# A transformer block and a graph attention on one core: three small attention products put side by side behind the up projection

## The chip, the cores and the metric

The kernel runs on one core of a Trainium2 chip. The metric is the device time of one launch in microseconds (us). Five engines of the core take part, each with its own queue of instructions in program order: TensorE (PE in the rows; its weight loads are PEld), VectorE (DVE), ScalarE (ACT), GpSimd (POOL), and SyncE (SP), which issues the DMAs. They meet only through semaphores.

## What is computed

128 sequences of 64 positions and 256 features go through two layers. All is float32; large products are made in pieces (below).

```python
# layer 0, per sequence
x_mod = rms(x) * (1 + scale_msa) + shift_msa
q, k, v = split(x_mod @ qkv_w)                   # 16 heads of 16
q, k = rope(rms(q) * lnq_w), rope(rms(k) * lnk_w)
attn = softmax(q @ k.T / 4)                      # 64 x 64 per head
x = x + gate_msa * (attn @ v @ proj_w + proj_b)
h = rms(x) * (1 + scale_mlp) + shift_mlp
x = x + gate_mlp * ((silu(h @ w1_w) * (h @ w3_w)) @ w2_w)   # 704 wide
# layer 1
sf = concat(x, where(x.sum(-1) == 0, 0, cond)) @ W_self.T + b_self
for d in range(2):                               # two directions
    aff = q1 @ k1.T / 4                          # keys: the first 20 positions
    w = softmax(where(mask, aff, NEG) + label_bias)
    out += w @ kv @ Wout[d] + bout[d]
y = x + relu(sf + out)
```

## The kernel before, in words

The 8192 rows are cut into 32 blocks of 256 positions (4 sequences); in most steps a block has two tiles `t` of 128 positions. Each engine runs a hand-written list of steps, `ORDER` (line 80), once per iteration of a loop over blocks. An entry `(a, step, n)` means: do part `n` of `step` for block `m + a`. So one iteration works on four blocks at once: `a = 3` is the youngest (norm and qkv), `a = 2` its first attention, `a = 1` projection and MLP, `a = 0` the graph attention, called the second attention here (its functions end in 1). `run_steps` (line 151) writes out the first four and the last three iterations and loops over the others. A block's work goes through all engines: for `qkv`, for instance, TensorE makes the product, ScalarE squares q and k (`qk_sq`) and copies v (`vb`), VectorE makes the two rotary products `qs` and `qc`, sums the squares, and adds `qr`.

Products of full precision take two parts of each operand, made as high (ScalarE copy to fp32r: `nh`, `gh`, `aoh`) and low part (the difference, on GpSimd: `nl`, `gl`; `aol` on VectorE). `linear` (line 483) writes their matmuls, so that their rows all have line 486.

Three kinds of TensorE work use a part of the array. `mix` (line 612; rows L622) multiplies transposed probabilities of the first attention with `v`, in tiles of 64 columns, 32 matmuls for each `t`. `mix1` (line 797; rows L806) does this for the second attention in tiles of 32 columns, also 32. `score`, `score1` and `v1` are tiled too and are not touched. Probabilities come from VectorE and ScalarE, are transposed by TensorE (`probs_t`, L607; `probs_t1`, L792), and copied to SBUF by ScalarE: to `pT0` for the first attention and to `pT1` for the second, one buffer each, used for both tiles in turn.

PSUM has 8 banks; `BANK` (line 72) says which product goes to which. Before a product overwrites a bank, TensorE waits for those who read what was in it (`wait_free`, line 139: a list of signals, each with a block offset and a count; the first whose block exists is waited for).

Other steps that the prediction names: TensorE `mixT` (L631, transposes the mixed values, the last but one step of an iteration), `heads` (L570, transposes q and k), `self` (the second layer's linear map, whose low part reads `nl` from `x2_split`), `mlp_down` in two parts. VectorE `mix` (L1162 reciprocal and L1165, divides by the sums), `qkv` (L1118, L1120, L1124, twice L1130), `mlp_up` (L1192, L1195, L1197, L1201), `mix1` (L1276), `edges` (L1221), `rope_scale` (L1135), `out` (L1282), `rope` (L1141), `mlp_down` (L1206, writes `x`). ScalarE `mlp_split` (L926, writes `gh`), `rope_scale` (L886, a square root, for which it loads a table). GpSimd `mlp_down` (L1360, adds to `x`), `heads` (L1327, `kbd`), `x2_split` (L1315, `nl`), `mlp_up` (L1315, `gl`). GpSimd's list ends `mlp_down`, `heads` 0, `x2_split`, `heads` 1, and VectorE's begins `rope` 0, `rope` 1, `mlp_down`.

The functions that the diff touches, with their lines:

Of the kernel before, what the change touches and what calls it, by code (L numbers as in the profile page):

```python
# [27 lines left out]
P = 128  # L28
# [45 lines left out]
    "mix": (5, 6), "q1": (4, 6), "score": 0, "score1": 0, "mixT": 6, "proj": 2, "norm1": 7, "up": (6, 4, 6),  # L74
# [10 lines left out]
        (1, "mlp_up", 1), (3, "qkv", 0), (0, "probsT1", 0), (2, "mix", 1), (3, "qkv", 1), (0, "mix1", 0),  # L85
        (0, "probsT1", 1), (1, "mlp_up", 2), (0, "mix1", 1), (1, "mlp_down", 0), (1, "mlp_down", 1), (2, "mixT", 0),
# [9 lines left out]
        (1, "mlp_up", 1), (2, "mix", 1), (3, "qkv", 0), (3, "qkv", 1), (1, "mlp_up", 2), (0, "mix1", 0),  # L96
# [8 lines left out]
        (0, "probsT1", 0), (3, "qkv", 0), (1, "mlp_split", 1), (3, "qkv", 1), (0, "probsT1", 1), (1, "mlp_up", 2),  # L105
# [64 lines left out]
def build_program(nc, d):  # L170
    with ExitStack() as ctx:
# [67 lines left out]
        pT0, pT1 = pT[:, 0, :, :], pT[:, 1, :, :]  # L239
# [242 lines left out]
        def _(pe):  # L482
# [129 lines left out]
            def mix(m, t):  # L612
# [3 lines left out]
                if t == 0:  # L616
                    wait_free(pe, m, (pT_a, 0, 1))
                elif t == 1:
                    wait_free(pe, m, (z_silu, -1, 1), (normed[0], 1, 1))
# [16 lines left out]
            def proj(m, n):  # L636
                first_use(m, "proj")
                wait(pe, mixed_hi, m, 1)
                wait_free(pe, m, (cos_part, 1, 1), (biased1, -2, 4))
# [7 lines left out]
            def mlp_up(m, n):  # L647
# [6 lines left out]
                for name, out in (("w1", z_ps[n]), ("w3", u_ps[n])):  # L654
# [8 lines left out]
                    elif (n, name) == (2, "w1"):  # L663
                        wait_free(pe, m, (mix_normed, 1, 2), (z_silu, 0, 1))
# [132 lines left out]
            def mix1(m, t):  # L797
# [5 lines left out]
                for j in range(NJ):  # L803
                    for s in range(2):
                        f = 32 * (j % 4)
                        last = nc.tensor.matmul(ao1_ps[f:f + 32, j // 4, t * P + s * S:t * P + (s + 1) * S],  # L806
                                                vb1[:, 2 * t + s, :, j], pT1[:, j, s * S:(s + 1) * S],
# [11 lines left out]
        def _(act):  # L819
# [47 lines left out]
            def qkv(m, t):  # L867
                wait(act, qkv_done, m, t + 1)
                qk_ps, v_ps = qkv_ps[t]

                wait(act, qk_sums, m, t)
                nc.scalar.activation(qk_sq[:, :, :, :].rearrange("p a h f -> p (a h f)"), qk_ps, ACT.Square)\
                    .then_inc(qk_squares.sem, 1)
                if t == 0:
                    wait_last(act, mixed, m)
                v = v_ps.rearrange("p (j h f) -> p j h f", h=2, f=DH)
# [561 lines left out]
```

## Time and profile before

| | |
|---|---|
| median of 3 runs | 1422.27 us (1420.46 to 1423.88) |
| span of the profiled execution, first to last instruction | 1416.1 us |
| what lies around the span, median less span | 6.2 us |
| granted TensorE clock, mean over the span | 0.977 |
| TensorE matmul busy | 1342.2 us (95%) |
| VectorE busy | 1135.2 us (80%) |
| ScalarE busy | 878.6 us (62%) |
| GpSimd busy | 712.1 us (50%) |
| DMA | 56.19 MB, mean 40 GB/s |

The timed executions and the profiled one are different executions; the span is what the rows below come from. Busy TensorE is the union of its matmuls, whose ends are modelled. The granted clock is at full speed from about the fourth block to the last; the slices before it are partly at half of that. Busy shares say how full an engine is, not whether something waits for it: for this the rows of a single block are needed.

### The profile page before, as it was taken

The numbers are of one execution on the slowest core, as the hardware profiler recorded it, in microseconds if no ns is written. First come the engines' busy times: TensorE is split into PE (matmuls) and PEld (weight loads), VectorE is DVE, ScalarE is ACT, GpSimd is POOL, SyncE is SP. The second block draws the span as 40 slices with busy tenths as digits, with TensorE's granted clock in tenths as the row PEclk, the third lists the DMA queues.
The fourth block names the chain that finished last, engine by engine and source line by source line (L and its number), as shares of the span: only waits on it lengthen the run. The fifth ranks groups of instructions, "written<-read, shape, count | busy, mean of one in ns | idle before, by whom it ended". The sixth has DMA issues, their size and how long they took to land.

```text
span 1416.1 us, 51305 instructions
## 1 busy us (share of the span) xinstructions
PE 1342.2 (95%) x20276; PEld 1229.1 (87%) x20276; DVE 1135.2 (80%) x2033; ACT 878.6 (62%) x1752; POOL 712.1 (50%) x612
## 2 busy tenths in 40 slices
PE   4679999999999999999999999999999999999985
PEld 3578899999998999999898999999999999999974
DVE  5667888888888888888888888888888888888753
ACT  4556666666666666666666666666666666656542
POOL 0235555455655544555555455555545555554541
PEclk8589999999999999999999999999999999999998
DMA  7001111010111101111110111111011111100100
GB/s 240 29 23 30 45 43 43 18 38 30 43 43 43 43 15 36 34 43 43 43 43 15 35 35 43 43 43 43 15 33 37 43 43 43 43 15 28 30 22 16
DMA packets 49827, 56.19 MB, mean 40 GB/s; under 512 B 4352, under 2 KB 47744, under 8 KB 49792
## 3 DMA queue, kind: packets, MB, share of 16 engines
q1 hardware_dynamic: 48944, 53.86, 12.1%
q10 hardware_dynamic: 848, 1.84, 0.4%
q8 instruction: 25, 0.41, 0.1%
q14 instruction: 10, 0.08, 0.0%
HBM read 47.03 MB, written 8.65 MB: 39 GB/s over the span
## 4 chain that ended last, share of the span: by engine, by line
PE 73%; issue 9%; POOL 7%; ACT 3%; DVE 1%; ACTq 0%; POOLq 0%; DVEq 0%
PE psum L486 39%; PE psum L607 5%; PE psum L622 5%; PE psum L728 4%; PE psum L792 4%; PE psum L758 4%; PE psum L775 3%; POOL nl L1315 3%; PE psum L587 3%; PE psum L806 2%; POOL gl L1315 2%; POOL kbd L1327 2%; ACT gh L926 1%; PE psum L534 1%; ACT qkT L892 1%
## 5 line engine op out<-in xcount | busy, mean ns | idle before, releaser
L1315 POOL TENSOR_TENSOR gl<-gf,gh 128x512 fp32r<-128x512 f32 x96 | 124.3, 1295 | 260.4 <-ACT gh L926 260.4
L486 PE MATMUL psum<-nh,w_lo 128*128 128x256 f32 x704 | 182.2, 289 | 0.0
L486 PE MATMUL psum<-nh,w_hi 128*128 128x256 f32 x704 | 176.8, 282 | 0.0
L1315 POOL TENSOR_TENSOR nl<-xn,nh 128x512 fp32r<-128x512 f32 x64 | 99.2, 1551 | 127.3 <-ACT nh L864 127.3
L486 PEld LDWEIGHTS psum<-nh,w_lo 128*128 128x128 f32 x704 | 132.8, 189 | 1.0 <-issue 1.0
L486 PEld LDWEIGHTS psum<-nh,w_hi 128*128 128x128 f32 x704 | 133.0, 189 | 0.0
L1379 POOL TENSOR_TENSOR e<-e,inv 128x640 f32<-128x640 f32 x64 | 82.0, 1282 | 87.6 <-DVE inv L1271 87.6
L486 PE MATMUL psum<-nl,w_hi 128*128 128x256 f32 x704 | 115.4, 282 | 0.0
L926 ACT ACTIVATE gh<-gf 128x512 fp32r<-128x512 f32 x96 | 60.3, 628 | 61.6 <-DVE gf L1201 60.8
L486 PEld LDWEIGHTS psum<-nl,w_hi 128*128 128x128 f32 x704 | 97.5, 188 | 0.0
L486 PE MATMUL psum<-qkv_lo,nh 128*128 128x512 f32 (+1 forms) x256 | 88.5, 356 | 2.8 <-ACT nh L864 2.8
L946 ACT ACTIVATE sf<-psum,colb 128x256 f32<-128x256 f32 x64 | 26.8, 470 | 103.3 <-PE psum L486 103.3
L1151 DVE TENSOR_REDUCE mx<-psum 128x16 f32<-128x1024 f32 x64 | 78.1, 1221 | 14.4 <-PE psum L587 14.1
L911 ACT ACTIVATE aoh<-psum 128x512 fp32r<-128x512 f32 x32 | 19.1, 598 | 109.2 <-PE psum L631 109.2
L486 PE MATMUL psum<-gh,w_lo 128*128 128x256 f32 x320 | 83.0, 290 | 1.3 <-ACT gh L926 1.3
L486 PE MATMUL psum<-qkv_hi,nh 128*128 128x512 f32 (+1 forms) x256 | 82.4, 343 | 0.0
L607 PE MATMUL psum<-ident,e 128*128 128x128 f32 x512 | 77.9, 289 | 4.3 <-ACT e L897 4.2
L1360 POOL TENSOR_TENSOR x<-x 128x512 f32<-128x512 f32 x32 | 41.5, 1296 | 78.2 <-DVE x L1206 78.2
L1327 POOL TENSOR_TENSOR kbd<-qkT,hmask 128x512 f32<-128x512 f32 x64 | 66.5, 1041 | 28.0 <-ACT qkT L892 28.0
L486 PE MATMUL psum<-gh,w_hi 128*128 128x256 f32 x320 | 79.6, 279 | 0.0
L1156 DVE TENSOR_TENSOR e<-psum,mx 128x1024 f32<-128x1024 f32 x64 | 78.0, 1218 | 1.3
L622 PEld LDWEIGHTS psum<-vb,pT 128*64 128x64 f32 x2048 | 66.6, 140 | 12.8 <-issue 12.5
(186 smaller groups left out, 4382.4 us busy)
## 6 DMA issues: line engine op xcount, KB each, us to landing
adj<-in_adj SPq DMA_DIRECT2D x32, 440.0 KB, 3.3
x_in<-in_x SPq DMA_DIRECT2D x32, 256.0 KB, 2.7
xn<-in_xT SPq DMA_DIRECT2D x32, 256.0 KB, 3.6
x_res<-in_xT SPq DMA_DIRECT2D x32, 256.0 KB, 3.7
out_T<-y SPq DMA_DIRECT2D x32, 256.0 KB, 2.2
e<-in_adaln ACTq DMA_DIRECT2D x2, 512.0 KB, 5.4
stage<-in_qkv SPq DMA_DIRECT2D x2, 384.0 KB, 5.0
pT<-in_w SPq DMA_DIRECT2D x2, 384.0 KB, 6.4
```

Of the source, the lines that this page charges most:

```text
L486: last = nc.tensor.matmul(out, lhsT, rhs, start=start and i == 0, stop=stop and i == len(terms) - 1)
L607: last = nc.tensor.transpose(pT_out[t][j // 4][:, j % 4, :], e0[t][:, 2 * pair(j):2 * pair(j) + 2, :].rearrange("p h s -> p (h s)"), ident ...
L622: last = nc.tensor.matmul(mix_ps[t][s * S:(s + 1) * S, j, :], pT0[:, j, s * S:(s + 1) * S], vb[:, t, s, j, :], start=True, stop=True, tile ...
L728: last = nc.tensor.matmul(k1_out[:, k, :].rearrange("p (b k) -> p b k", b=MB), wk1[:, c, k * P:(k + 1) * P], sf[:, c, :].rearrange("p (b s ...
L758: last = nc.tensor.matmul(v1_out[r * NKP:(r + 1) * NKP, b, :], kv[:, c, b, :], wo1[:, c, r * P:(r + 1) * P], start=c == 0, stop=c == DC - ...
L792: last = nc.tensor.transpose(pT1_out[t][j // 4][:, j % 4, :], e1[t][:, 2 * pair(j):2 * pair(j) + 2, :, :].rearrange("p h a k -> p (h a k)" ...
L926: nc.scalar.activation(gh[:, 2 * n:2 * n + 2, :], gf[:, :, :], ACT.Copy).then_inc(g_hi.sem, 1)
L1151: nc.vector.tensor_reduce(mx0_v, s_v[t], AX.X, ALU.max).then_inc(maxima.sem, 1)
L1156: nc.vector.tensor_tensor(e0_v[t], s_v[t], mx0_v.unsqueeze(3).to_broadcast([P, NG, 4, S]), ALU.subtract).then_inc(shifted_s.sem, 1)
L1315: return nc.gpsimd.tensor_tensor(out, full, hi.bitcast(F32), ALU.subtract)
L1327: nc.gpsimd.tensor_tensor(kbd[:, t, :, :, :, :].rearrange("p c s h k -> p (c s) h k"), qkT[t][:, 1, :, :].rearrange("p c (s k) -> p (c s) ...
L1379: nc.gpsimd.tensor_tensor(e_v, e_v, inv1[t][:, :].unsqueeze(2).to_broadcast([P, ND * H, NKV]), ALU.mult)\
```

## The change

In TensorE's list the second `mix` (tile 1 of the first attention) and both `mix1` move behind the last part of the up projection, so that the three follow each other. For this the transposed probabilities of the second attention get a second buffer, `mix` 1 writes bank 2 in place of bank 6, and the waits before reuse of banks follow. VectorE's `mix` 1 moves from before `qkv` to behind the last `mlp_up`. On ScalarE the copies of v leave `qkv` and become a step of their own, `values`: tile 0's stays behind `qkv` 0, tile 1's comes last in the list, since it may overwrite `vb` only when the `mix` of the block before has read it. There `qkv` 1 also changes places with `probsT1` 1.

```diff
@@ -71,7 +71,7 @@
 
 BANK = {
     "xT": 6, "qk": (2, 3), "v": (7, 1), "heads": (7, 5), "probsT": (5, 4, 4, 0), "probsT1": (0, 5, 4, 7),
-    "mix": (5, 6), "q1": (4, 6), "score": 0, "score1": 0, "mixT": 6, "proj": 2, "norm1": 7, "up": (6, 4, 6),
+    "mix": (5, 2), "q1": (4, 6), "score": 0, "score1": 0, "mixT": 6, "proj": 2, "norm1": 7, "up": (6, 4, 6),
     "gate": (3, 1, 0), "down": 1, "rowsum": 3, "self": 4, "k1": 5, "v1": 7, "mix1": 5,
 }
 
@@ -82,8 +82,8 @@
         (2, "heads", 1), (1, "proj", 0), (0, "self", 0), (0, "self_cond", 0), (2, "score", 0), (0, "k1", 0),
         (0, "q1", 0), (1, "norm1_mean", 0), (0, "q1", 1), (1, "norm1_apply", 0), (2, "probsT", 0),
         (3, "norm0_apply", 0), (0, "score1", 0), (0, "v1", 0), (2, "mix", 0), (2, "probsT", 1), (1, "mlp_up", 0),
-        (1, "mlp_up", 1), (3, "qkv", 0), (0, "probsT1", 0), (2, "mix", 1), (3, "qkv", 1), (0, "mix1", 0),
-        (0, "probsT1", 1), (1, "mlp_up", 2), (0, "mix1", 1), (1, "mlp_down", 0), (1, "mlp_down", 1), (2, "mixT", 0),
+        (1, "mlp_up", 1), (3, "qkv", 0), (0, "probsT1", 0), (3, "qkv", 1), (0, "probsT1", 1), (1, "mlp_up", 2),
+        (2, "mix", 1), (0, "mix1", 0), (0, "mix1", 1), (1, "mlp_down", 0), (1, "mlp_down", 1), (2, "mixT", 0),
         (3, "heads", 0),
     ],
     "DVE": [
@@ -93,7 +93,7 @@
         (3, "norm0_apply", 0), (3, "norm0_shift", 0), (0, "score1_bias", 0), (0, "score1_max", 0),
         (0, "score1_bias", 1), (0, "score1", 0), (2, "mix", 0), (0, "score1_max", 1), (0, "soft1", 0),
         (0, "soft1_inverse", 0), (1, "mlp_up", 0), (0, "score1", 1), (0, "soft1", 1), (0, "soft1_inverse", 1),
-        (1, "mlp_up", 1), (2, "mix", 1), (3, "qkv", 0), (3, "qkv", 1), (1, "mlp_up", 2), (0, "mix1", 0),
+        (1, "mlp_up", 1), (3, "qkv", 0), (3, "qkv", 1), (1, "mlp_up", 2), (2, "mix", 1), (0, "mix1", 0),
         (1, "edges", 0), (3, "rope_scale", 0), (0, "out", 0),
     ],
     "Activation": [
@@ -102,7 +102,8 @@
         (3, "norm0_mean", 0), (2, "score", 0), (0, "q1", 0), (0, "q1", 1), (2, "probsT", 0), (2, "score", 1),
         (1, "norm1_apply", 0), (0, "v1", 0), (3, "norm0_apply", 0), (1, "edges", 0), (0, "score1", 0),
         (2, "probsT", 1), (1, "mlp_up", 0), (1, "mlp_split", 0), (0, "score1", 1), (1, "mlp_up", 1),
-        (0, "probsT1", 0), (3, "qkv", 0), (1, "mlp_split", 1), (3, "qkv", 1), (0, "probsT1", 1), (1, "mlp_up", 2),
+        (0, "probsT1", 0), (3, "qkv", 0), (3, "values", 0), (1, "mlp_split", 1), (0, "probsT1", 1), (3, "qkv", 1),
+        (1, "mlp_up", 2), (3, "values", 1),
     ],
     "Pool": [
         (1, "proj", 0), (0, "self_split", 0), (3, "norm0_mean", 0), (1, "norm1_mean", 0), (1, "norm1_scale", 0),
@@ -236,7 +237,7 @@
         inv0 = [sb(f"inv0_{i}", [P, NJ, 2]) for i in range(TILES)]
         aon = [sb(f"aon{i}", [P, NJ, 2, DH]) for i in range(TILES)]
         pT = sb("pT", [P, 2, NJ, P])
-        pT0, pT1 = pT[:, 0, :, :], pT[:, 1, :, :]
+        pT0, pT1 = pT[:, 0, :, :], [pT[:, 1, :, :], sb("pT1_1", [P, NJ, P])[:, :, :]]
         aoh = sb("aoh", [P, DC, MT], F32R)
         aol = sb("aol", [P, DC, MT], F32R)
 
@@ -616,7 +617,7 @@
                 if t == 0:
                     wait_free(pe, m, (pT_a, 0, 1))
                 elif t == 1:
-                    wait_free(pe, m, (z_silu, -1, 1), (normed[0], 1, 1))
+                    wait_free(pe, m, (cos_part, 1, 1), (biased1, -2, 4), (shifted_s, 0, 2))
                 for j in range(NJ):
                     for s in range(2):
                         last = nc.tensor.matmul(mix_ps[t][s * S:(s + 1) * S, j, :], pT0[:, j, s * S:(s + 1) * S],
@@ -636,7 +637,7 @@
             def proj(m, n):
                 first_use(m, "proj")
                 wait(pe, mixed_hi, m, 1)
-                wait_free(pe, m, (cos_part, 1, 1), (biased1, -2, 4))
+                wait_free(pe, m, (mix_normed, 0, 2))
                 for o in both:
                     linear(proj_ps[:, o, :], high_terms("proj", out_chunks[o], aoh, both), o == 0, False)
                 wait(pe, mixed_lo, m, 1)
@@ -661,7 +662,7 @@
                     elif (n, name) == (1, "w3"):
                         wait_free(pe, m, (biased1, -1, 4), (shifted_s, 1, 2))
                     elif (n, name) == (2, "w1"):
-                        wait_free(pe, m, (mix_normed, 1, 2), (z_silu, 0, 1))
+                        wait_free(pe, m, (z_silu, 0, 1))
                     elif (n, name) == (2, "w3"):
                         wait_free(pe, m, (pT1_a, -1, 1), (pT_b, 1, 2))
                     for c, w, j in chunks[name]:
@@ -804,7 +805,7 @@
                     for s in range(2):
                         f = 32 * (j % 4)
                         last = nc.tensor.matmul(ao1_ps[f:f + 32, j // 4, t * P + s * S:t * P + (s + 1) * S],
-                                                vb1[:, 2 * t + s, :, j], pT1[:, j, s * S:(s + 1) * S],
+                                                vb1[:, 2 * t + s, :, j], pT1[t][:, j, s * S:(s + 1) * S],
                                                 start=True, stop=True, tile_position=(0, f))
                 last.then_inc(mixed1.sem, 1)
 
@@ -866,14 +867,14 @@
 
             def qkv(m, t):
                 wait(act, qkv_done, m, t + 1)
-                qk_ps, v_ps = qkv_ps[t]
-
                 wait(act, qk_sums, m, t)
-                nc.scalar.activation(qk_sq[:, :, :, :].rearrange("p a h f -> p (a h f)"), qk_ps, ACT.Square)\
+                nc.scalar.activation(qk_sq[:, :, :, :].rearrange("p a h f -> p (a h f)"), qkv_ps[t][0], ACT.Square)\
                     .then_inc(qk_squares.sem, 1)
-                if t == 0:
-                    wait_last(act, mixed, m)
-                v = v_ps.rearrange("p (j h f) -> p j h f", h=2, f=DH)
+
+            def values(m, t):
+                wait(act, qkv_done, m, t + 1)
+                wait(act, mixed, m, t + 1 - TILES)
+                v = qkv_ps[t][1].rearrange("p (j h f) -> p j h f", h=2, f=DH)
                 for s in range(2):
                     for h in range(2):
                         last = nc.scalar.activation(vb[h * S:(h + 1) * S, t, s, :, h * DH:(h + 1) * DH],
@@ -983,14 +984,14 @@
 
             def probs_t1(m, t):
                 wait(act, pT1_ps, m, 2 * t + 1)
-                wait(act, mixed1, m, t)
-                nc.scalar.activation(pT1[:, 0:4, :], pT1_out[t][0], ACT.Copy).then_inc(pT1_a.sem, 1)
+                wait(act, mixed1, m, t + 1 - TILES)
+                nc.scalar.activation(pT1[t][:, 0:4, :], pT1_out[t][0], ACT.Copy).then_inc(pT1_a.sem, 1)
                 wait(act, pT1_ps, m, 2 * t + 2)
-                nc.scalar.activation(pT1[:, 4:8, :], pT1_out[t][1], ACT.Copy).then_inc(pT1_b.sem, 1)
+                nc.scalar.activation(pT1[t][:, 4:8, :], pT1_out[t][1], ACT.Copy).then_inc(pT1_b.sem, 1)
 
             run_steps(act, "Activation", {
                 "norm0_mean": norm0_mean, "norm1_mean": norm1_mean, "norm0_apply": norm_apply(0),
-                "norm1_apply": norm_apply(1), "qkv": qkv, "rope_scale": rope_scale, "heads": heads, "score": score, "probsT": probs_t, "mixT": mix_t,
+                "norm1_apply": norm_apply(1), "qkv": qkv, "values": values, "rope_scale": rope_scale, "heads": heads, "score": score, "probsT": probs_t, "mixT": mix_t,
                 "mlp_up": mlp_up, "mlp_split": mlp_split, "x2_split": x2_split, "self": self_feat, "self_split": self_split, "keys": keys, "q1": q1, "v1": v1,
                 "score1": score1, "probsT1": probs_t1, "edges": edges,
             }, {("norm0_mean", 0): gate_and_mlp_mods} | {step: partial(high_parts, *pieces) for step, pieces in HIGH_PARTS.items()})
```

## Rows read from the trace of the kernel before

**Rows 1.** Timeline, TensorE: first and last `mixT` of 28 (columns in the first line).

```profile
start us, us, engine line op out<-in xcount [idle before <-releaser]
191.68 0.66 PE L631 MATMUL psum<-ident,aon 128*128 128x128 f32 x4
...
1309.65 0.55 PE L631 MATMUL psum<-ident,aon 128*128 128x128 f32 x3
```

**Rows 2.** Who waited for whom, whole span: us in total, times, longest us.

```profile
PEld psum L486 <- POOL nl L1315: 9.6, 30, 0.3
...
DVE x L1206 <- PE psum L696: 2.8, 3, 1.2
```

**Rows 3.** Timeline, TensorE, around `self`.

```profile
646.89 0.27 PE L696 MATMUL psum<-gl,w_hi 64*128 64x256 f32 x1
...
651.40 0.28 PE L486 MATMUL psum<-nh,self_hi 128*128 128x256 f32 x1
651.78 0.39 PE L486 MATMUL psum<-nl,ones_r 128*128 128x256 f32 x1
```

**Rows 4.** Timeline, GpSimd, `x2_split` and what it stands behind.

```profile
648.19 1.30 POOL L1360 TENSOR_TENSOR x<-x 128x512 f32<-128x512 f32 x1 [2.46 <-DVE x L1206]
...
650.45 1.28 POOL L1315 TENSOR_TENSOR nl<-x,nh 128x512 fp32r<-128x512 f32 x1
```

**Rows 5.** Timeline, VectorE, second half of a block.

```profile
633.57 0.69 DVE L1201 TENSOR_TENSOR gf<-gf,psum 128x512 f32<-128x512 f32 x1
635.62 0.26 DVE L1162 RECIPROCAL inv<-psum 128x16 f32<-128x16 f32 x1 [1.36 <-PE psum L622]
...
636.25 0.68 DVE L1118 TENSOR_TENSOR qs<-psum,sinw 128x512 f32<-128x512 f32 x1
...
638.04 1.36 DVE L1130 TENSOR_TENSOR qr<-qc,qs 128x256 f32<-128x256 f32 x2
639.43 0.69 DVE L1118 TENSOR_TENSOR qs<-psum,sinw 128x512 f32<-128x512 f32 x1
...
641.23 0.75 DVE L1130 TENSOR_TENSOR qr<-qc,qs 128x256 f32<-128x256 f32 x2
...
642.86 0.69 DVE L1201 TENSOR_TENSOR gf<-gf,psum 128x512 f32<-128x512 f32 x1
...
647.43 0.68 DVE L1206 TENSOR_TENSOR x<-psum,mods 128x512 f32<-128x512 f32 x1
```

**Rows 6.** Timeline, GpSimd, a `nl` and the `gl` of `mlp_up` 1.

```profile
621.99 1.68 POOL L1315 TENSOR_TENSOR nl<-xn,nh 128x512 fp32r<-128x512 f32 x1 [1.85 <-ACT nh L864]
...
637.49 1.29 POOL L1315 TENSOR_TENSOR gl<-gf,gh 128x512 fp32r<-128x512 f32 x1 [1.36 <-ACT gh L926]
```

**Rows 7.** Timeline, VectorE, `norm1_shift`.

```profile
621.84 0.69 DVE L1107 TENSOR_TENSOR xn<-xn,mods 128x512 f32<-128x512 f32 x1
```

**Rows 8.** Timeline, ScalarE, 634 to 644 us.

```profile
634.11 0.60 ACT L987 ACTIVATE pT<-psum 128x512 f32<-128x512 f32 x1 [1.96 <-PE psum L792]
...
635.08 0.61 ACT L872 ACTIVATE qk_sq<-psum 128x512 f32<-128x512 f32 x1
635.61 1.14 ACT L879 ACTIVATE vb<-psum 64x128 f32<-64x128 f32 x4
636.78 0.63 ACT L926 ACTIVATE gh<-gf 128x512 fp32r<-128x512 f32 x1
...
642.20 1.28 ACT L886 ACT_TABLE_LOAD   x1
```

**Rows 9.** Timeline, TensorE, `mix` 1, `qkv` 1 and the second `mix1`.

```profile
634.44 1.13 PE L622 MATMUL psum<-vb,pT 128*64 128x34 f32 x32
635.50 0.50 PE L486 MATMUL psum<-qkv_lo,nh 128*128 128x512 f32 x1
635.83 0.39 PE L486 MATMUL psum<-qkv_hi,nh 128*128 128x512 f32 x1
636.06 0.39 PE L486 MATMUL psum<-qkv_lo,nh 128*128 128x512 f32 x1
...
641.69 0.81 PE L806 MATMUL psum<-pT,vb 128*32 128x64 f32 x32
```

## The prediction, made before the changed kernel ran

> **What bounds the kernel now.** The busy shares of the page name TensorE (95%), and its chain of waits lies mostly on TensorE lines. Both are an average, so I went to one block in the steady stretch. The loop is regular: `mixT` starts at 191.68 and 27 blocks later at 1309.65 [rows 1], so a block takes 1117.97 / 27 = 41.41 us. Next I asked the table of waits for something that TensorE waits for in every block. It is one place: 30 waits, 9.6 us in all, for the `nl` that GpSimd makes in `x2_split` [rows 2]. In the block shown the last matmul before it starts at 651.40 and the next at 651.78, where matmuls of this shape follow each other at 0.12: TensorE loses 0.26 us there [rows 3]. The reader is to see who is late. GpSimd's `nl` ends at 650.45 + 1.28 = 651.73; it stands straight behind `kbd` and the addition `x`, which started at 648.19, released by VectorE's `x` [rows 4]. VectorE's `x` (L1206) starts at 647.43 and ends at 648.11 [rows 5], while TensorE had given it its input at 646.89 + 0.27 = 647.16 [rows 3]. It waited for TensorE in 3 blocks only [rows 2]: otherwise it is late because VectorE is still busy with its own queue. From 638.04 to 647.43 VectorE has no idle time worth a row. So in the second half of the block the order is: VectorE's queue, then GpSimd x, kbd, nl, then TensorE. TensorE itself is not the bound there, it has 0.26 us to spare.
>
> What sets VectorE's queue? Before it there is idle time, 634.26 (633.57 + 0.69) to 635.62, ended by the second `mix` [rows 5]. But the bound is not the mix. The first `qr` of tile 0 (L1130) starts at 638.04 and the pair takes 1.36, where the same pair of tile 1 takes 0.75 [rows 5]: 0.6 us longer. GpSimd is then in `gl`, 637.49 to 638.78 [rows 6], and both read two tensors in SBUF. The reverse case is there too: the `nl` at 621.99 takes 1.68 [rows 6], against 1.28 for the same operation at 650.45 [rows 4], when VectorE's `xn` (two SBUF inputs) had started before it, at 621.84 [rows 7]. So whoever starts second waits for the first. The `qr` can't finish before some 638.78 + 0.3, however early it is reached. Hence the chain of a block is: ScalarE `qk_sq`, four `vb` copies, `gh` [rows 8], GpSimd `gl`, VectorE `qr`, VectorE's queue to `x`, GpSimd to `nl`, TensorE. The second `mix` of VectorE (from 635.62 to the start of `qs` at 636.25: 0.63 us) lies ahead of that hold-up, and is free now.
>
> The Trainium skill, "SBUF — State Buffer", Who interferes with whom, states this as a rule: a VectorE instruction with two SBUF inputs and a GpSimd instruction that reads SBUF exclude each other, the first one for its whole length. The trace agrees (1.36 against 0.75). By the rule a block of the new order costs the 0.60 worked out below; if the two only slowed each other in proportion, it would be the 0.20 of rival 1.
>
> **What the change does, part by part.**
>
> *TensorE order.* No instruction is added or removed. The small-tile groups `mix` (columns of 64) and the two `mix1` (columns of 32) no longer stand alone between full-array work. Leaving a tile costs: the first full matmul behind `mix` is followed after 635.83 - 635.50 = 0.33, the next ones after 0.23 [rows 9], so 0.1 us. Entering is taken as the same. Six edges become two and one change of tile size, four fewer: 4 x 0.1 = 0.4 us per block off TensorE (estimate; between 0, if the three groups drain alike, and 0.5). It comes in the part of the block where TensorE already waits 0.26 us for the other chain, so it only lengthens that wait: worth 0.
>
> *Waits of TensorE.* The mix to bank 2 waits for `cos_part` and `proj` for `mix_normed`, both done long before. `qkv` of tile 1 now comes some 1.06 us earlier (the mix that stood before it, 634.44 to 635.50 [rows 9]), so at about 634.4; it waits for VectorE's product that ends at 634.26 [rows 5]: 0 to 0.1 us, inside the spare time. `mlp_down` part 0 waits for `v_kept` of tile 1, next paragraph.
>
> *ScalarE.* `values` splits the `vb` copies off. Tile 0's stand where they stood, so `gh` and GpSimd's `gl` don't move. Tile 1's (1.14 us, as [rows 8]) now stand behind the second mix, in front of the table load for the square root, the last `gh` and its `gl`, for which `mlp_down` part 1 waits. Before, the up projection ended at 641.69 [rows 9]. Now it ends without a mix (1.06) and a mix1 (0.73) before it, at about 639.9; the mix ends 1.13 later, 641.0; the copies run 641.1 to 642.2, and the table load was at 642.20 anyway [rows 8]. Cost 0. `mlp_down` part 0 is reached about 642.3: 0 to 0.1 us. If this cover failed the whole 1.14 would show (a rival).
>
> *VectorE.* `mix` moves from before `qkv` to behind the last `mlp_up`. Tile 0's `qs` needs only `qk_sq`, which ends 635.08 + 0.61 = 635.69, so it starts at 635.72 to 635.85 in place of 636.25. `qr` is reached 1.79 later (638.04 - 636.25), at 637.51 to 637.64. GpSimd's `gl` starts at 637.49, still ahead, though by as little as 0.02 us. So `qr` is held to the same 638.78, and `qs` of tile 1 stays at 639.43. The 0.4 to 0.5 us won are lost in the hold. Everything to L1201 at 642.86 stays; then 0.63 us of mix are new on the path, and `mix1`, `edges`, `rope_scale`, `out`, both `rope` and `x` are each 0.63 later: `x` at 648.06. Up to 0.09 can come back at L1197, which follows L1195 without the usual overlap because its tanh came late. I take +0.60. `rope` is late too, and `heads` waits for it, which removes TensorE's lead at once.
>
> *The rest.* GpSimd's x, kbd and nl follow `x` without slack: +0.60 at TensorE's `nl`. Everything from there to `probsT1` of tile 0 is ordered by TensorE and keeps its distances. No DMA is moved; the store waits for `out`, 0.6 later, and its buffer is wanted a block later: 0. The second buffer of transposed probabilities lifts ScalarE's wait for `mix1`, which lies on no bound: 0.
>
> **Sum.** 27 blocks x 0.60 = 16.2. The few blocks ahead of 191.68, and the last, which have no `qkv`, are bound by TensorE or by loading, and keep the 0.3 to 0.4 us of edges: -1.5 together (estimate). 1416.1 + 16.2 - 1.5 = 1430.8 of span; the median of the runs is 6.2 above the span of the profiled execution, so 1437.0. Unless the clock or another bound enters, the likeliest case holds 1432 to 1441.
>
> **Rivals.**
>
> 1. *Half of it.* VectorE's `qr` gets in ahead of `gl`, or isn't held. The next bound is ScalarE's `qk_sq` of tile 1: `gh` ends at 637.41, two `pT` copies cost 635.08 - 634.11 = 0.97 [rows 8], then 0.61: 638.9 and `qs` at 639.0 in place of 639.43. Cost 0.63 - 0.43 = 0.20 per block: 5.4 - 1.5, so 1426. For it: the margin is 0.02 to 0.15. Against: between the two `qr`, GpSimd would get its turn and hold the second.
>
> 2. *Faster: the 0.4 us of edges arrive.* That decides if the late `x` isn't what holds TensorE, that is, if VectorE's queue has more than 0.63 + 0.4 us of slack behind 639.43. Then 27 x -0.4 = -11, 1411. For it: VectorE is busy 80% only and idle for 1.36 us in this stretch. Against: 30 waits in 31 blocks, behind a VectorE that has no gap from 638.04 on [rows 2, 5]. The Trainium skill, "TensorEngine Tiling (Array Packing)", Key Properties, says that changing the tiling mode drains TensorE, which speaks for this rival; the 0.33 against 0.23 agrees that an edge costs something, but not that it is on the path.
>
> 3. *Nothing.* Both effects small, or the 0.63 hidden by VectorE operations that now run without overlap losses: 1420 to 1425.
>
> 4. *Worse.* The copies of tile 1 delay the last `gh` by up to 1.14 and `mlp_down` with it, on top: up to 0.9 us per block in place of 0.6, 1446. It needs the mix to end a microsecond later than I reckon.
>
> **How the numbers follow.** 0.2% (2.8 us) is about what a measurement of this kernel can tell from no change. Chances: forecast 0.70, half 0.07, worse 0.05, so slower 0.82; nothing 0.07; faster 0.11. The predicted time is 1437. The range 1424 to 1446 takes in forecast, half and worse, 0.80 with what the forecast loses at its edges.
>
> **What the profile after would show.** Right: a block of 42.0 us; `qs` of tile 0 some 0.4 us sooner behind its `qk_sq`; the first `qr` still ending with GpSimd's `gl`; the second `mix` without idle before it; TensorE's wait for `nl` grown from 0.26 to some 0.9 us; `mix1` straight behind `mix`. Wrong: `x` on VectorE waiting for TensorE in every block (rival 2), a pair of `qr` of 0.75 in tile 0 (rival 1), or TensorE waiting for `gl` of the last part by more than 0.3 us (rival 4).

## The result, and the profile after

The changed kernel takes 1442.34 us (median of 4 runs, 1442.02 to 1446.09), the kernel before, measured beside it, 1423.08 (4 runs, 1420.46 to 1425.49). The ratio is 1.0146, with a 95% interval of 1.0126 to 1.0166: slower, by 19.3 us or 1.5%. 1437.0 was forecast, with a range of 1424 to 1446. The profiled execution has a span of 1440.2 us at the same mean granted clock as before (0.976 against 0.977).

Line numbers are one higher than before from the buffer's line on. The block first, `mixT` at both ends of the same 27 blocks (timeline of TensorE after: start, us, engine, line, operation, out<-in, tile, form, count):

```profile
194.12 0.66 PE L632 MATMUL psum<-ident,aon 128*128 128x128 f32 x4
...
1327.42 0.66 PE L632 MATMUL psum<-ident,aon 128*128 128x128 f32 x4
```

(1327.42 - 194.12) / 27 = 41.97 us, against 41.41 [rows 1]. The 27 blocks take 1133.30 - 1117.97 = 15.3 us more, 0.57 each.

VectorE in the second half of a block, in the same view as [rows 5]:

```profile
642.24 0.69 DVE L1202 TENSOR_TENSOR gf<-gf,psum 128x512 f32<-128x512 f32 x1
644.48 0.69 DVE L1119 TENSOR_TENSOR qs<-psum,sinw 128x512 f32<-128x512 f32 x1 [1.55 <-ACT qk_sq L871]
...
646.27 1.81 DVE L1131 TENSOR_TENSOR qr<-qc,qs 128x256 f32<-128x256 f32 x2
648.12 0.69 DVE L1119 TENSOR_TENSOR qs<-psum,sinw 128x512 f32<-128x512 f32 x1
...
649.92 0.75 DVE L1131 TENSOR_TENSOR qr<-qc,qs 128x256 f32<-128x256 f32 x2
...
651.55 0.69 DVE L1202 TENSOR_TENSOR gf<-gf,psum 128x512 f32<-128x512 f32 x1
652.15 0.25 DVE L1163 RECIPROCAL inv<-psum 128x16 f32<-128x16 f32 x1
652.44 0.42 DVE L1166 TENSOR_TENSOR aon<-psum,inv 128x256 f32<-128x256 f32 x1
...
656.74 0.68 DVE L1207 TENSOR_TENSOR x<-psum,mods 128x512 f32<-128x512 f32 x1
```

and GpSimd beside it (the first row answers to [rows 6], the others to [rows 4]):

```profile
646.17 1.30 POOL L1316 TENSOR_TENSOR gl<-gf,gh 128x512 fp32r<-128x512 f32 x1 [1.37 <-ACT gh L927]
...
657.50 1.32 POOL L1361 TENSOR_TENSOR x<-x 128x512 f32<-128x512 f32 x1 [3.21 <-DVE x L1207]
...
659.77 1.29 POOL L1316 TENSOR_TENSOR nl<-x,nh 128x512 fp32r<-128x512 f32 x1
```

and ScalarE's copy and square of tile 0 (before: [rows 8]):

```profile
642.87 0.60 ACT L988 ACTIVATE pT<-psum 128x512 f32<-128x512 f32 x1 [2.06 <-PE psum L793]
...
643.84 0.60 ACT L871 ACTIVATE qk_sq<-psum 128x512 f32<-128x512 f32 x1
```

Read it from the top. The idle time ahead of `qs` is now ended by ScalarE's `qk_sq` and no longer by the second mix. `qr` is reached at 646.27, 1.79 behind `qs`. GpSimd's `gl` runs 646.17 to 647.47, it had started 0.10 before. The pair of `qr` takes 1.81, and `qs` of tile 1 comes at 648.12, 1.95 behind the start of `gl`; before it was 639.43 - 637.49 = 1.94 [rows 5, 6]. So what the mix's absence gave was lost in the hold to 0.01 us. From `qs` of tile 1 to `x` it takes 656.74 - 648.12 = 8.62, before 647.43 - 639.43 = 8.00 [rows 5]: +0.62, and in it stand a reciprocal and a multiply of the second mix (652.15 to 652.78), without idle time ahead of them.

TensorE at the other end of the chain, and behind the up projection:

```profile
648.37 1.13 PE L623 MATMUL psum<-vb,pT 128*64 128x34 f32 x32
649.42 1.39 PE L807 MATMUL psum<-pT,vb 128*32 128x64 f32 x64
...
659.53 0.50 PE L487 MATMUL psum<-nh,ones_r 128*128 128x256 f32 x2 [0.51 <-ACT nh L939]
...
660.71 0.28 PE L487 MATMUL psum<-nh,self_hi 128*128 128x256 f32 x1
661.12 0.50 PE L487 MATMUL psum<-nl,ones_r 128*128 128x256 f32 x2
```

`mix1` stands straight behind `mix`, one group of 64. `nl` ends at 659.77 + 1.29 = 661.06, and the matmul that reads it starts at 661.12. TensorE loses 661.12 - 660.71 - 0.12 = 0.29 us there, as before (0.26), and 0.51 at `nh`, which it did not wait for in this place before. The waits of the whole span say the same (waiting, line <- releaser: us in total, times, longest):

```profile
PEld psum L487 <- ACT nh L939: 23.8, 30, 3.0
...
PEld psum L571 <- DVE qr L1142: 12.2, 27, 5.5
...
PEld psum L487 <- POOL nl L1316: 9.8, 30, 0.3
...
PEld psum L487 <- POOL gl L1316: 6.1, 29, 0.5
```

The wait for `nl` is as it was [rows 2]. The one for `nh`, which ScalarE makes of the same late `x`, is 23.8 us in 30 waits, where before it was 3.8 in 5. `heads` waits for VectorE's rope 12.2 us in 27 waits, where before it was 12.5 in 2: the sum is no larger, but in most of the 27 blocks there is now a wait of about 0.2 us, and before there was none. Both are the late VectorE queue of the forecast.

### The profile page after: what moved, and what is told of

The parts are those of the page before. It is cut to its first block, busy times and chain, and to the rows that moved or that the text cites. A ratio compares the mean times of both kernels' runs of the same rounds, so it can differ in the third digit from the quotient of the medians.

```text
span 1440.2 us, 51310 instructions
## 1 busy us (share of the span) xinstructions
PE 1349.1 (94%) x20276; PEld 1228.8 (85%) x20276; DVE 1145.2 (80%) x2033; ACT 880.9 (61%) x1752; POOL 710.8 (49%) x612
## 4 chain that ended last, share of the span: by engine, by line
PE 65%; issue 12%; POOL 8%; ACT 7%; DVE 1%; POOLq 0%; ACTq 0%; DVEq 0%
PE psum L487 35%; PE psum L759 5%; PE psum L608 4%; PE psum L623 4%; PE psum L729 4%; PE psum L793 4%; PE psum L776 3%; POOL gl L1316 3%; POOL nl L1316 3%; ACT L887 3%; PE psum L588 2%; ACT vb L880 2%; POOL kbd L1328 2%; ACT gh L927 1%; PE psum L535 1%
## 5 line engine op out<-in xcount | busy, mean ns | idle before, releaser
L1119 DVE TENSOR_TENSOR qs<-psum,sinw 128x512 f32<-128x512 f32 x64 | 44.3, 691 | 54.0 <-ACT qk_sq L871 52.6
L880 ACT ACTIVATE vb<-psum 64x128 f32<-64x128 f32 x256 | 70.3, 275 | 24.8 <-PE psum L623 22.5
L1131 DVE TENSOR_TENSOR qr<-qc,qs 128x256 f32<-128x256 f32 x128 | 79.9, 664 | 0.0
```

What stands on the lines that cost most here:

```text
L880: last = nc.scalar.activation(vb[h * S:(h + 1) * S, t, s, :, h * DH:(h + 1) * DH], v[s * S:(s + 1) * S, :, h, :], ACT.Copy)
L1131: nc.vector.tensor_tensor(qr[t][:, :, :, a * half:(a + 1) * half], qc[:, :, :, a * half:(a + 1) * half], qs[:, :, :, (1 - a) * half:(2 - a ...
```

## The experiments

Each kernel is the kernel before or the changed one with the edit shown. "Block" is the mean of the 27 blocks between the fourth and the 31st `mixT` in its profile. "Way" is the time from ScalarE's first copy `pT` of tile 0 (L987 in the kernel before, 634.11 in [rows 8]) to the start of VectorE's `x` (L1206, 647.43 in [rows 5]), the median over these blocks, in none of which it is more than 0.03 off. The kernels before beside them had medians of 1421.0 to 1422.2.

| kernel | median us (lowest to highest, runs) | ratio to before, 95% | block us | way us |
|---|---|---|---|---|
| before | | 1 | 41.41 | 13.32 |
| changed | 1442.34 (1442.02 to 1446.09, 4) | 1.0146 [1.0126, 1.0166] | 41.97 | 13.88 |
| before_mix_twice | 1421.50 (1419.18 to 1425.61, 10) | 1.0013 [0.9998, 1.0029] | 41.41 | 13.32 |
| after_mix_twice | 1455.11 (1452.97 to 1456.51, 4) | 1.0244 [1.0213, 1.0275] | 42.43 | 14.32 |
| before_split_first | 1419.65 (1416.13 to 1425.84, 12) | 0.9993 [0.9980, 1.0005] | 41.40 | 13.31 |
| after_split_first | 1434.99 (1433.08 to 1439.49, 4) | 1.0104 [1.0069, 1.0140] | 41.75 | 13.67 |
| after_qkv_first | 1441.38 (1439.15 to 1445.49, 4) | 1.0139 [1.0109, 1.0169] | 41.98 | 13.87 |
| after_both_first | 1432.35 (1428.70 to 1433.96, 6) | 1.0079 [1.0063, 1.0096] | 41.58 | 13.49 |
| after_split_between | 1430.49 (1423.33 to 1432.13, 7) | 1.0052 [1.0031, 1.0073] | 41.57 | 13.49 |
| buffer_and_mix1_only | 1423.93 (1418.14 to 1427.82, 12) | 1.0007 [0.9993, 1.0020] | 41.43 | 13.25 |
| buffer_mix1_split_first | 1411.01 (1406.19 to 1411.69, 6) | 0.9917 [0.9898, 0.9935] | 41.00 | 12.83 |
| after_groups_apart | 1450.32 (1449.70 to 1450.75, 4) | 1.0202 [1.0180, 1.0224] | 42.30 | 14.23 |
| groups_apart_qkv_first | 1446.67 (1442.11 to 1447.21, 4) | 1.0170 [1.0143, 1.0198] | 42.06 | 13.98 |
| after_one_buffer | 1561.53 (1560.70 to 1562.37, 2) | 1.0986 [1.0956, 1.1016] | 45.86 | 17.91 |

Block less way, from `x` to the next block's copy, is 28.07 to 28.11 us in eleven of the fourteen kernels, the kernel before and the changed one among them, although their blocks lie between 41.40 and 42.43. So what the change costs in a block, 0.57 us, lies between that copy and `x`, and not in TensorE's or GpSimd's part behind it. The three others are after_one_buffer (27.95) and the two that move `mix1` alone (28.18 and 28.17); why the latter are 0.1 us longer isn't shown.

**Is the second mix free ahead of the hold, and does it cost in full behind it?** Both kernels do its reciprocal and its multiply once more, into a tile that nothing reads.

```diff
                 wait(dve, mix_normed, m, t + 1 - TILES)
+                if t == 1:
+                    nc.vector.reciprocal(spare[:, :, :, 0], mix_ps[t][:, :, 2 * DH:2 * DH + 2])
...
+                if t == 1:
+                    nc.vector.tensor_tensor(spare[:, :, :, :], mix_ps[t][:, :, 0:2 * DH].rearrange("p j (h f) -> p j h f", h=2),
+                                            inv0[t][:, :, :].unsqueeze(3).to_broadcast([P, NJ, 2, DH]), ALU.mult)
```

before_mix_twice:

> The kernel before with VectorE's work for the second mix done twice (a second reciprocal and a second multiply, into a spare tile), some 0.52 us more per block, in its old place ahead of qkv. Theory (the first qr of tile 0 is held by GpSimd's gl, and what stands ahead of the hold is free): qr is reached 0.52 us later, still 0.1 before it could run, so 0 per block, 1421 to 1426. Rival (VectorE is the bound all through, its work counts wherever it stands): 27 x 0.52 = 14 us more, 1437.

after_mix_twice:

> The changed kernel with the same doubling, now behind the hold. Theory: all of it shows, 27 x 0.52 = 14 us on 1442, so 1456, a block of 42.5. Rival (the loss of the change is in TensorE's or ScalarE's new order, not in VectorE's queue): 1442 to 1444.

The same two instructions cost nothing in the one (41.41) and 0.46 us per block in the other (12.3 over the 27; the medians are 12.8 apart, 1455.11 against 1442.34, from two sets of runs). VectorE of before_mix_twice shows how:

```profile
633.98 0.26 DVE L1164 RECIPROCAL spare<-psum 128x16 f32<-128x16 f32 x1 [1.32 <-PE psum L623]
...
635.06 0.68 DVE L1119 TENSOR_TENSOR qs<-psum,sinw 128x512 f32<-128x512 f32 x1
...
636.84 0.92 DVE L1131 TENSOR_TENSOR qr<-qc,qs 128x256 f32<-128x256 f32 x2
637.80 0.69 DVE L1119 TENSOR_TENSOR qs<-psum,sinw 128x512 f32<-128x512 f32 x1
```

GpSimd there (the added lines shift the numbers):

```profile
635.85 1.29 POOL L1321 TENSOR_TENSOR gl<-gf,gh 128x512 fp32r<-128x512 f32 x1 [1.32 <-ACT gh L927]
```

The mix takes 635.06 - 633.98 = 1.08 in place of 0.63, and the pair of `qr` 0.92 in place of 1.36. The 0.45 us come out of the hold, which had 0.6 to give. This is the main reading of the forecast, and the runs show it.

**The hold itself.** ScalarE splits `gh` ahead of `qkv` 0, so that GpSimd's `gl` is over when `qr` comes.

```diff
-        (0, "probsT1", 0), (3, "qkv", 0), (3, "values", 0), (1, "mlp_split", 1), (0, "probsT1", 1), (3, "qkv", 1),
+        (0, "probsT1", 0), (1, "mlp_split", 1), (3, "qkv", 0), (3, "values", 0), (0, "probsT1", 1), (3, "qkv", 1),
```

> The changed kernel, ScalarE's mlp_split 1 (gh) moved ahead of qkv 0, so that GpSimd's gl runs before VectorE reaches qr. Theory (port held): the first qr takes 0.4 instead of 1.5 us; the next bound is qk_sq of tile 1 behind the two pT copies; VectorE's x comes 0.4 sooner, a block of about 41.55, 27 x 0.43 = 12 us less than 1442, so 1431. Rival (qr is slow for another reason, such as its place behind qk_ss): it stays near 1.5 and gh's 0.5 us ahead of qk_sq makes a block 42.0 to 42.5, 1442 to 1455.

The same exchange in the kernel before:

> The kernel before with mlp_split 1 ahead of qkv 0 on ScalarE. Theory: the hold goes (qr pair from 1.36 to 0.75 us), but TensorE's mlp_up 2 ends so late that VectorE's L1197 waits for its tanh: at most 0.09 us of a block come back, 1419 to 1423. Rival (the hold alone sets the block): 0.59 less per block, 27 x 0.59 = 16, so 1407.

Timeline of VectorE in after_split_first, and under it GpSimd's:

```profile
643.96 0.69 DVE L1119 TENSOR_TENSOR qs<-psum,sinw 128x512 f32<-128x512 f32 x1 [2.07 <-ACT qk_sq L871]
...
645.75 0.76 DVE L1131 TENSOR_TENSOR qr<-qc,qs 128x256 f32<-128x256 f32 x2
646.88 0.69 DVE L1119 TENSOR_TENSOR qs<-psum,sinw 128x512 f32<-128x512 f32 x1 [0.37 <-ACT qk_sq L871]
```

GpSimd:

```profile
643.72 1.30 POOL L1316 TENSOR_TENSOR gl<-gf,gh 128x512 fp32r<-128x512 f32 x1
```

The hold is gone: `gl` starts 2.03 us ahead of `qr`, and the pair takes 0.76. The block gets 0.22 us shorter, not the 0.4 expected: `gh` now pushes `qk_sq` back (idle 2.07 in place of 1.55 ahead of `qs`), and `qs` of tile 1 waits 0.37 for its own `qk_sq`. In the kernel before the same exchange gives nothing; its next wait is another one (VectorE):

```profile
633.66 0.75 DVE L1130 TENSOR_TENSOR qr<-qc,qs 128x256 f32<-128x256 f32 x2
...
637.85 0.41 DVE L1197 SCALAR_TENSOR_TENSOR gf<-th,psum 64x256 f32<-64x256 f32 x1 [0.40 <-ACT th L921]
```

The pair is 0.75 there too, and 0.40 of what it gives is lost at L1197, where ScalarE's tanh of the last up projection comes late.

**ScalarE's order around tile 1.** after_qkv_first puts `qkv` 1 ahead of `probsT1` 1, after_both_first does this and the exchange above; after_split_between puts `gh` between `qk_sq` and the copies of tile 0, with `qkv` 1 ahead too.

```diff
-        (0, "probsT1", 0), (3, "qkv", 0), (3, "values", 0), (1, "mlp_split", 1), (0, "probsT1", 1), (3, "qkv", 1),
+        (0, "probsT1", 0), (3, "qkv", 0), (3, "values", 0), (1, "mlp_split", 1), (3, "qkv", 1), (0, "probsT1", 1),
```

> The changed kernel, ScalarE's qkv 1 (qk_sq of tile 1) put back ahead of probsT1 1, gl left where it is. Theory: qk_sq of tile 1 is wanted only behind the held qr, so nothing changes, 1440 to 1445, a block of 41.98. Rival (ScalarE's new order of these two steps is what costs): back towards 1430.

```diff
+        (0, "probsT1", 0), (1, "mlp_split", 1), (3, "qkv", 0), (3, "values", 0), (3, "qkv", 1), (0, "probsT1", 1),
```

> The changed kernel with both moves on ScalarE: mlp_split 1 ahead of qkv 0, and qkv 1 ahead of probsT1 1. Theory: the hold is gone and qk_sq of tile 1 follows qk_sums at once, so VectorE's queue is 1.1 us shorter; then TensorE, ScalarE's last gh and GpSimd's gl are close together, a block of 41.0 to 41.1, 1417 to 1420, a little under the kernel before. Rival (TensorE's order needs the 41.4 in any case): a block of 41.4, 1427.

```diff
+        (0, "probsT1", 0), (3, "qkv", 0), (1, "mlp_split", 1), (3, "values", 0), (3, "qkv", 1), (0, "probsT1", 1),
```

> The changed kernel with ScalarE's order qk_sq of tile 0, gh (mlp_split 1), the v copies of tile 0, qk_sq of tile 1, probsT1 1. Theory: gh no longer delays qk_sq and GpSimd's gl is over when VectorE reaches qr, so qs of tile 0 starts as early as in the changed kernel, the pair of qr takes 0.75, qs of tile 1 comes 1.1 us sooner: a block of 40.9 to 41.1 in place of 41.98, 27 x 0.95 = 26 us less than 1442, so 1415 to 1419, below the kernel before. Rival (the v copies, now later, hold probsT1 1 on TensorE through the bank they share and that becomes the bound): 41.3 to 41.5, 1424 to 1430.

after_qkv_first moves nothing (41.98): its pair of `qr` still takes 1.81, so an earlier `qk_sq` for tile 1 finds VectorE held. after_both_first takes 41.58, 0.17 less than the exchange alone. I had expected 41.0 to 41.1 and had left out that `gh` stands 0.5 us in front of `qk_sq`. after_split_between avoids that and still misses, 41.57. Its rows of VectorE and GpSimd name what is next:

```profile
650.38 1.18 DVE L1283 SCALAR_TENSOR_TENSOR y<-sf,x 128x512 f32<-128x512 f32 x1
```

GpSimd:

```profile
649.71 1.30 POOL L1316 TENSOR_TENSOR gl<-gf,gh 128x512 fp32r<-128x512 f32 x1 [7.06 <-ACT gh L927]
```

`out` reads two tensors in SBUF as well, took 0.62 in the changed kernel, and takes 1.18 here: VectorE is now so early that it meets the last `gl`. A hold that is taken away at one pair comes back at the next. The two misses have one size: after_both_first loses 0.51 at `qs` (2.06 idle in place of 1.55) and takes 0.66 for `out`, after_split_between loses nothing at `qs` and 0.56 at `out`, and both have a way of 13.49. VectorE in after_both_first:

```profile
638.86 0.69 DVE L1119 TENSOR_TENSOR qs<-psum,sinw 128x512 f32<-128x512 f32 x1 [2.06 <-ACT qk_sq L871]
...
648.44 0.66 DVE L1283 SCALAR_TENSOR_TENSOR y<-sf,x 128x512 f32<-128x512 f32 x1
```

The rival that was named for after_split_between is in its trace too: TensorE's transposes of tile 1 wait for the copies of v, 11.1 us in 28 waits, about 0.4 a block, and the changed kernel has no such wait. But after_split_first has the same 11.1 in 28, after_both_first 11.5 in 29, and what their blocks have over the kernel before (0.34, 0.17, 0.16) is what their ways have over it (0.35, 0.17, 0.17). So it doesn't set these blocks; whether it would be the next bound isn't shown.

**TensorE's groups.** buffer_and_mix1_only is the kernel before with the second buffer and `mix1` 0 moved beside `mix1` 1; the second mix stays. buffer_mix1_split_first adds ScalarE's exchange. TensorE's part of the edit (the buffer's lines are those of the change):

```diff
-        (1, "mlp_up", 1), (3, "qkv", 0), (0, "probsT1", 0), (2, "mix", 1), (3, "qkv", 1), (0, "mix1", 0),
-        (0, "probsT1", 1), (1, "mlp_up", 2), (0, "mix1", 1), (1, "mlp_down", 0), (1, "mlp_down", 1), (2, "mixT", 0),
+        (1, "mlp_up", 1), (3, "qkv", 0), (0, "probsT1", 0), (2, "mix", 1), (3, "qkv", 1),
+        (0, "probsT1", 1), (1, "mlp_up", 2), (0, "mix1", 0), (0, "mix1", 1), (1, "mlp_down", 0), (1, "mlp_down", 1), (2, "mixT", 0),
```

> One part of the change alone: the second buffer of transposed probabilities, and mix1 0 moved beside mix1 1 behind mlp_up 2; the first attention's second mix, its bank and all of VectorE's and ScalarE's order as before. Theory: VectorE's queue is unchanged, so the saved tile changes only lengthen TensorE's wait for nl, 0 per block, 1421 to 1426. Rival (tile changes are on the path): two edges and a drain, 0.2 to 0.3 us per block, 1414 to 1417.

> The last one with mlp_split 1 ahead of qkv 0 as well. Theory: the hold is gone, mlp_up 2 ends 0.8 us sooner so that the tanh is in time, and the second mix stays ahead of qkv: VectorE's queue is 0.6 us shorter and TensorE or ScalarE's last gh becomes the bound, a block of 40.9 to 41.1, 1409 to 1414, the fastest of all. Rival (another bound right behind): 41.3, 1420.

Grouping alone is worth nothing (41.43). What TensorE saves turns into waiting: its weight loads wait 10.6 us in 30 waits for `nh` (before 3.8 in 5), 4.7 in 27 for the last `gl` (before 0.8 in 1) and 9.9 for `nl` (before 9.6), about 11 us more in all. That is 0.4 a block, where the expectation put the saved edges at 0.2 to 0.3. Grouping and exchange together are worth 0.41 us per block, where the exchange alone gave 0.01 (before_split_first): each lets the other's gain through. VectorE of buffer_mix1_split_first:

```profile
635.71 0.75 DVE L1130 TENSOR_TENSOR qr<-qc,qs 128x256 f32<-128x256 f32 x2
636.61 0.69 DVE L1118 TENSOR_TENSOR qs<-psum,sinw 128x512 f32<-128x512 f32 x1
...
639.50 0.41 DVE L1197 SCALAR_TENSOR_TENSOR gf<-th,psum 64x256 f32<-64x256 f32 x1
...
644.61 0.68 DVE L1206 TENSOR_TENSOR x<-psum,mods 128x512 f32<-128x512 f32 x1
```

and ScalarE's tanh of the last up projection, in before_split_first first:

```profile
633.84 0.60 ACT L872 ACTIVATE qk_sq<-psum 128x512 f32<-128x512 f32 x1 [1.01 <-DVE qk_ss L1124]
...
637.43 0.38 ACT L921 ACTIVATE th<-psum 64x256 f32<-64x256 f32 x1 [0.59 <-PE psum L486]
```

the same rows of buffer_mix1_split_first:

```profile
635.89 0.60 ACT L872 ACTIVATE qk_sq<-psum 128x512 f32<-128x512 f32 x1 [1.00 <-DVE qk_ss L1124]
...
638.77 0.38 ACT L921 ACTIVATE th<-psum 64x256 f32<-64x256 f32 x1
```

The pair of `qr` is 0.75, and L1197 waits for no tanh (1.4 us in 2 waits in the whole span, against 12.4 in 30 in before_split_first). In before_split_first that tanh waits 0.59 for TensorE and starts 3.59 us behind the second `qk_sq`; here, with a `mix1` less in front of the up projection, 2.88 and without a wait. This kernel, at 1411.01, is faster than before_split_first, buffer_and_mix1_only and the kernel before.

The other direction takes a group out of the changed kernel, `mix1` 0 back behind `qkv` 1; groups_apart_qkv_first has ScalarE's `qkv` 1 ahead of `probsT1` 1 as well.

```diff
-        (1, "mlp_up", 1), (3, "qkv", 0), (0, "probsT1", 0), (3, "qkv", 1), (0, "probsT1", 1), (1, "mlp_up", 2),
-        (2, "mix", 1), (0, "mix1", 0), (0, "mix1", 1), (1, "mlp_down", 0), (1, "mlp_down", 1), (2, "mixT", 0),
+        (1, "mlp_up", 1), (3, "qkv", 0), (0, "probsT1", 0), (3, "qkv", 1), (0, "mix1", 0), (0, "probsT1", 1), (1, "mlp_up", 2),
+        (2, "mix", 1), (0, "mix1", 1), (1, "mlp_down", 0), (1, "mlp_down", 1), (2, "mixT", 0),
```

> The changed kernel with mix1 0 back between qkv 1 and probsT1 1 on TensorE, so that the small-tile groups are not all together; everything else as changed. Theory (tile changes are off the path): as the changed kernel within 0.2%, 1440 to 1444, a block of 41.98, TensorE's wait for nl or heads shorter by the 0.3 us that the edges cost. Rival (standing together brings something): 0.2 to 0.3 us per block more, 1448 to 1450.

> The kernel with the groups apart (mix1 0 between qkv 1 and probsT1 1), and on ScalarE qkv 1 ahead of probsT1 1. Two readings of its extra 8 us: (a) mix1 0 pushes probsT1 1 back by 0.8 us, ScalarE's copies wait for it, and qk_sq of tile 1 waits behind the copies; then the swap takes all of it away, a block of 41.98 as in the changed kernel, 1440 to 1444. (b) The groups apart cost TensorE time that is on the path; then the swap does nothing, a block of 42.3, 1448 to 1451.

ScalarE in after_groups_apart:

```profile
649.91 0.60 ACT L988 ACTIVATE pT<-psum 128x512 f32<-128x512 f32 x1 [0.68 <-PE psum L793]
...
650.88 0.61 ACT L871 ACTIVATE qk_sq<-psum 128x512 f32<-128x512 f32 x1
```

VectorE:

```profile
651.61 0.69 DVE L1119 TENSOR_TENSOR qs<-psum,sinw 128x512 f32<-128x512 f32 x1 [0.40 <-ACT qk_sq L871]
```

after_groups_apart is 0.33 us per block slower than the changed kernel. The theory (nothing) missed, and the rival's time of 1448 to 1450 came out. ScalarE's copies of tile 1 wait 0.68 for TensorE's later transposes, `qk_sq` stands behind them, and VectorE's `qs` waits 0.40. With `qkv` 1 ahead, 0.24 of the 0.33 go: they were this queue, and not the tile edges. The last 0.09 is `out` again, which takes 0.72 there in place of 0.62 and starts at 660.89, while the last `gl` runs from 659.78 to 661.07.

**The second buffer.** One buffer in the changed order.

```diff
-        pT0, pT1 = pT[:, 0, :, :], [pT[:, 1, :, :], sb("pT1_1", [P, NJ, P])[:, :, :]]
+        pT0, pT1 = pT[:, 0, :, :], [pT[:, 1, :, :]] * 2
...
-                wait(act, mixed1, m, t + 1 - TILES)
+                wait(act, mixed1, m, t)
```

> The changed kernel with one buffer of transposed probabilities for both tiles, so that ScalarE's copies of tile 1 wait for mix1 0. Theory: mix1 0 now ends some 3.8 us after the copies were made, and qk_sq of tile 1 is queued behind them on ScalarE, and VectorE's qkv 1 behind that: 3.6 us per block, 27 x 3.6 = 97, about 1540. Rival (only mix1 1 waits for its copies): 1 us per block, 1470.

ScalarE in after_one_buffer:

```profile
696.15 0.60 ACT L988 ACTIVATE pT<-psum 128x512 f32<-128x512 f32 x1 [4.34 <-PE psum L807]
```

ScalarE's copy of tile 1 waits 4.34 us for `mix1` 0, and the block takes 45.86, 3.9 more than the changed kernel, where 3.6 was expected. The time, 1561.53, misses the 1540 by more: 27 x 3.9 = 105 of the 119 us are in the 27 blocks, and the other 14 outside them weren't reckoned with. The new order needs the buffer; what the buffer alone is worth in the old order no run shows, and buffer_and_mix1_only, which has it, is no faster.

## Why the prediction was right, point by point

- **VectorE's queue as the bound, the mix free ahead of the hold: right.** The way from `qs` 1 to `x` is 0.62 longer, and the mix gone ahead of the hold brought nothing: +0.57 per block where +0.60 was put. before_mix_twice and after_mix_twice show both halves. The Trainium skill, "SBUF — State Buffer", Who interferes with whom, has the two engines exclude each other, the first for its whole length. The runs agree with it: reached 0.55, 0.99 and 0.10 us behind the start of `gl` (the kernel before, before_mix_twice, the changed one), the pair took 1.36, 0.92 and 1.81 and ended 0.61 or 0.62 us behind the end of `gl` each time. A slowing in proportion, which the prediction priced with rival 1, would not give that.
- **`qs` of tile 0 sooner by 0.4, and lost: right.** The idle ahead of it is ended by `qk_sq`, behind whose start it now stands 0.64 (644.48 - 643.84) in place of 1.17 (636.25 - 635.08 [rows 5, 8]), 0.53 sooner, and `qs` 1 stands 1.95 behind the start of `gl`, as before.
- **Tile edges worth 0: right.** buffer_and_mix1_only removes two of them, TensorE waits longer instead, and the time stays. The Trainium skill, "TensorEngine Tiling (Array Packing)", Key Properties, says that a change of mode drains the array. No run here shows what such a drain is worth once VectorE is no longer late: in buffer_mix1_split_first it can't be told from the sooner tanh.
- **The copies of tile 1 behind the second mix cost nothing: right.** TensorE waits for the last `gl` 6.1 us in 29 waits, 0.2 each (before 0.8 in 1), under the 0.3 that was named as the bound for rival 4, and what stands behind `x` is no longer than before (block less way 28.09 in both).
- **Up to 0.09 back at L1197: wrong, and without weight.** It was read as an overlap lost to a late tanh. In the changed kernel the instruction stands 0.42 behind L1195's (651.01 - 650.59), as before, and in buffer_mix1_split_first, where the tanh is in time, 0.43. Nothing came back: the way from `qs` 1 to `x` grew by 0.62 of the 0.63.
- **TensorE's wait for `nl` grown to 0.9: right in amount, wrong in place.** 0.51 + 0.29 = 0.80, but the growth shows at `nh`, a step ahead on the same chain. The step "TensorE itself is not the bound there" looked at one wait only; `nh` had its slack used up first.
- **The term -1.5 for the blocks outside the 27: mis-sized, and of the wrong sign.** 19.3 measured less 15.3 is +4.0, with an interval of 2.6 to 8.3 from that of the ratio. The forecast's difference was 14.7 (16.2 - 1.5); the measured one is 4.6 larger, 0.9 less from the 27 blocks and 5.5 more from this term, and so the time lies above the likeliest range of 1432 to 1441. A part is shown: the last block, without `qkv`, from the 31st `mixT` to the next, takes 38.5 us in the changed kernel and 36.7 before, 1.8 more. 0.7 of it comes ahead of the first transposes below (26.04 against 25.34 behind the 31st `mixT`): the late `x` of the block before holds up `nh` here too, by 0.58 us. The other 1.1 is this; TensorE, before:

```profile
1334.99 1.04 PE L792 MATMUL psum<-ident,e 128*128 128x128 f32 x8
1335.96 1.13 PE L622 MATMUL psum<-vb,pT 128*64 128x34 f32 x32
1337.02 0.81 PE L806 MATMUL psum<-pT,vb 128*32 128x64 f32 x32
1337.76 1.09 PE L792 MATMUL psum<-ident,e 128*128 128x128 f32 x8
```

after:

```profile
1353.46 1.04 PE L793 MATMUL psum<-ident,e 128*128 128x128 f32 x8
1355.73 1.09 PE L793 MATMUL psum<-ident,e 128*128 128x128 f32 x8 [1.23 <-POOL e L1380]
```

and GpSimd after:

```profile
1354.41 1.27 POOL L1380 TENSOR_TENSOR e<-e,inv 128x640 f32<-128x640 f32 x1 [0.78 <-DVE inv L1272]
```

The transposes of tile 1 now stand straight behind those of tile 0 and wait 1.23 us for GpSimd's probabilities, which end at 1354.41 + 1.27 = 1355.68; with no `qkv` 1 between them, the removed groups had been the cover. The two kernels that put `mix1` 0 back there take 37.8 and 37.6 us for this block, 0.7 and 0.9 less than the same kernels without it (38.5). I had looked only at what those blocks save. In the five profiles with the second mix in its old place this block takes 36.7 to 37.2 us, in the eight others with two buffers 37.6 to 39.0.
- **The distance from span to median: 6.2 us was carried over, 2.1 measured.** Within one execution the time stands 1.7 to 3.0 us above the span in all the executions on record of this and the other kernels. The 6.2 was the distance of a quick profiled execution from the median of others, and not something that lies around a span: 1416.1 is low among the spans of the kernel before that are on record (1414.2 to 1423.9). The span came out at 1440.2, 9.4 above the 1430.8 of the forecast. Behind the last `mixT` the profile after has 74.3 us at a mean granted clock of 0.84, that of before 69.8 at 0.91. Over the eleven other profiles without after_one_buffer this stretch takes 71.9 to 74.7, at 0.81 to 0.88, whichever order they have. So the 4.5 us are mostly the clock of one execution, and they are about what the spans' difference (24.1) has over that of the medians (19.3); I count them to no step of the change.
- **What stays open.** The first stretch, up to the fourth `mixT`, took 191.68 us before and 194.12 after, but 187.4 to 195.4 over the profiles with the second mix in its place and 192.6 to 199.8 over those with it moved: the two overlap, and the rest of the +4.0, some 2.2, can't be settled by them.

## What to carry to other kernels

Before an operation is moved, find on each queue where the engine is held up next: work ahead of a hold is free as long as the hold has time left, and the same work behind it costs in full, here 0 and 12.8 us for the same two instructions. Ask it of the first and last blocks too, where the work that covered a wait may be missing. To see which stretch sets a loop, take the same two rows in every kernel and compare the time between them with the block: here block less way stayed within 0.04 us over eleven kernels. When a removed hold gives less than its length, look for the next pair or the next late input (here `out` against the last `gl`, a `qk_sq`, a tanh); two edits worth nothing each can be worth 0.8% together.

## What the runs showed of the hardware

- A VectorE operation with two SBUF inputs that starts while GpSimd works takes up to GpSimd's rest on top: a pair of `qr` 1.81 us against 0.75, when `gl` had started 0.10 before it. It is so for SCALAR_TENSOR_TENSOR too: `out` 1.18 against 0.62. An operation with one input isn't held: `edge_n` (L1222) starts at 653.56 in the changed kernel, 0.56 behind the start of a `gl` (653.00, 1.30), and takes 1.05, and in after_split_between, where `gl` starts inside it, 1.06.
- Two instructions added to the busier VectorE queue (0.45 us per block, 27 blocks) left the time where it was, 1.0013 [0.9998, 1.0029], in a place where VectorE was going to be held.
